# Attention with a decaying causal mask inside a one-core layer: wider transposed scores, wider products with V, a mask at the diagonal tiles alone

## The reference, cut to what matters

```python
Q, K, V = ...                                  # 2 x 16 heads, each 512 x 16
S = jnp.einsum('hid,hjd->hij', K, Q) * SCALE   # row i by K, column j by Q
delta = idx[:, None] - idx[None, :]
decay = jnp.where(delta < 0, 0.0, -delta.astype(jnp.float32) ** ALPHA)   # ALPHA = 1
S = jnp.where(delta < 0, -jnp.inf, S) + decay
C = jax.nn.softmax(S, axis=-1)
attn = jnp.einsum('hij,hjd->hid', C, V)
```

## Time and profile before

| | us |
|---|---|
| median of 3 runs | 376.57 (376.19 to 376.78) |
| span of the profiled execution | 374.3 |
| PE, DVE, ACT, POOL busy | 261.6, 257.6, 167.8, 142.4 |

### The profile page before, as it was taken

The page is one execution under the profiler, slowest core; times in us unless marked ns, Lnnn a source line. Parts: engine busy times, 40 slices in busy tenths (PEclk is TensorE's granted clock), DMA queues, the critical chain, the costliest instruction groups (busy, mean ns, idle before and its releaser), DMA issues.

```text
span 374.3 us, 7052 instructions
## 1 busy us (share of the span) xinstructions
PE 261.6 (70%) x2080; PEld 200.1 (53%) x2080; DVE 257.6 (69%) x833; ACT 167.8 (45%) x412; POOL 142.4 (38%) x212
## 2 busy tenths in 40 slices
PE   1715652999993179769999999998619429999900
PEld 0504541998982058515445455466418319898800
DVE  5798463587874787797788888446676406787726
ACT  2850352455554126325666776767142105565400
POOL 6390684177875004372000000000007733877730
PEclk9975887699998559955999999999956859999965
DMA  5999593544530704853333221000002232545227
GB/s 158 389 227 188 165 331 116 183 151 139 159 109 3 223 1 121 250 157 103 87 87 87 73 60 43 1 2 2 1 2 77 104 116 87 164 132 166 82 91 246
DMA packets 33931, 45.66 MB, mean 122 GB/s; under 512 B 5869, under 2 KB 27475, under 8 KB 33896
## 3 DMA queue, kind: packets, MB, share of 16 engines
q1 hardware_dynamic: 29304, 36.25, 34.6%
q0 software_dynamic: 4592, 8.98, 7.0%
HBM read 28.06 MB, written 20.61 MB: 130 GB/s over the span
## 4 chain that ended last, share of the span: by engine, by line
PE 34%; DMA 19%; POOL 15%; DVE 13%; issue 10%; SPq 5%; ACT 4%; POOLq 0%; DVEq 0%; ACTq 0%
PE bank L295 15%; POOL slots_x L512 8%; DMA slots_x<-zeros 7%; POOL results L526 5%; PE bank L922 5%; DMA xb<-slots_x 5%; PE bank L880 4%; DVE bank L1275 3%; DMA yg<-results 2%; DMA stk_q<-parts_d 2%; PE bank L831 2%; PE bank L901 2%; SPq L414 2%; DVE res L1197 1%; PE bank L740 1%
## 5 line engine op out<-in xcount | busy, mean ns | idle before, releaser
L526 POOL DMA_INDIRECT results<-ysb,yi x62 | 61.0, 984 | 31.3 <-DVE ysb L1178 17.1
L1275 DVE CUSTOM_DVE_ANT_0 bank<-bank,dec 128x512 f32<-128x512 f32 (+3 forms) x128 | 60.6, 510 | 14.6 <-PE bank L880 13.6
L512 POOL DMA_INDIRECT slots_x<-xn,slot x32 | 31.8, 993 | 33.6 <-DVE slot L1118 12.9
L586 ACT ACTIVATE sg<-bank 128x128 f32<-128x128 f32 x78 | 21.6, 277 | 51.3 <-PE bank L295 51.3
L880 PE MATMUL bank<-stk_q,stk_k 96*128 96x512 bf16 (+3 forms) x128 | 39.3, 340 | 6.8 <-DVE mmax L1275 4.8
L1166 DVE TENSOR_TENSOR xT_l<-bank,xT_h 128x256 fp32r<-128x256 f32 x62 | 26.4, 425 | 24.0 <-ACT xT_h L625 23.9
L295 PE MATMUL bank<-wh,xT_h 128*128 x124 | 41.8, 337 | 0.8 <-DVE xT_l L1166 0.8
L625 ACT ACTIVATE xT_h<-bank 128x256 fp32r<-128x256 f32 x62 | 23.8, 384 | 38.8 <-PE bank L831 37.9
L831 PE MATMUL bank<-ident,xb 128*128 128x128 f32 x124 | 25.8, 293 | 20.4 <-DMA xb<-slots_x 19.8
L712 ACT ACTIVATE ct<-bank,dec 128x512 f32<-128x512 f32 x64 | 34.8, 581 | 7.7 <-PE bank L901 7.5
L504 POOL COPY xn<-to_row 128x4 int32<-128x4 int32 x8 | 2.3, 289 | 93.7 <-DVE xn L1059 93.7
(11 more groups left out here) (173 smaller groups left out, 729.9 us busy)
## 6 DMA issues: line engine op xcount, KB each, us to landing
xb<-slots_x SPq DMA_DIRECT2D x62, 128.5 KB
w_raw<-in_experts SPq DMA_DIRECT2D x17, 384.0 KB, 6.4
yg<-results SPq DMA_DIRECT2D x16, 256.0 KB, 4.5
slots_x<-zeros SPq DMA_DIRECT2D x1, 3983.5 KB, 27.6
parts_d<-part SPq DMA_DIRECT2D x6, 384.0 KB, 2.8
stk_k<-parts_d SPq DMA_DIRECT2D x8, 192.0 KB, 3.4
stk_q<-parts_d SPq DMA_DIRECT2D x8, 192.0 KB, 3.5
res<-in_x SPq DMA_DIRECT2D x4, 256.0 KB, 3.7
```

What stands on the lines that cost most here:

```text
L512: pool.indirect_dma_start(slots_x, where, xn[:, t, :], None)\
L526: pool.indirect_dma_start(results, where, ysb[c % RING][:], None, bounds_check=4 * N - 1, oob_is_err=False).then_inc(s_ys[c % RING], 16)
L1275: dve.tensor_tensor_reduce(s_i, s_i, dec[:, SEQ - w:SEQ], 1.0, NEG, ALU.add, ALU.max, mmax[g % 2][:, n % G * QT + i:n % G * QT + i + 1])\
```

## The change

The decay comes from six rows in place of three, chosen so that they hold for every pair of tiles: three with the place in a tile and the tile number of i, three with those of j. So a transposed tile row can be one matmul that starts at its own diagonal tile: 512, 384, 256 and 128 columns. Entries above the diagonal are hidden by a second matmul that adds `hide` (0 or -3e38) to the diagonal tiles alone. The steps of a head are now tile row 0 (bank 2); rows 3 and 1 (bank 3); row 2 (bank 4). The columns that the array takes for a head are the same: 512 + 512 + 512 + 256 = 1792 before, and (512 + 128) + (128 + 384 + 256) + (256 + 128) = 1792 now, in 7 matmuls in place of 8. The banks' sizes and the three exponentials stay; none has a bias from memory now.

`ct` now holds a tile row's diagonal tile and what is behind it side by side, so a product with V is one matmul for each tile row and head: 4 pieces of 512, 384, 256 and 128 columns, in place of 7, at three places of the loop in place of six. The columns are the same: 1280 for each head.

The rows are built at the start in two small tiles, by four instructions on POOL (`place_k`, `place_q`) and four DMAs that write into them and wait for POOL (`s_place`); `hide` takes two more instructions on POOL. Of ACT's three copies at the end of the first shared expert two are left. The stack is 104 rows high (`STD`) in place of 101, and `decay_rows` writes 6 and 8 rows in place of 3 and 5.

```diff
-    STD = STM + 3
+    STD = STM + 6
...
+        t_tiles = [(0,), (3, 1), (2,)]
+        ct_at = {0: 0, 3: 512, 1: 640, 2: 1024}
...
-            at = SEQ + 1
-            sp.dma_start(masks_s[:, 0:P], masks[:, at:at + P]).then_inc(s_msk, 16)
-            sp.dma_start(masks_s[0:3, P:P + SEQ], masks[0:3, at + P:at + P + SEQ]).then_inc(s_msk, 16)
-            sp.dma_start(masks_s[32:37, P:P + SEQ], masks[3:8, at + P:at + P + SEQ]).then_inc(s_msk, 16)
+            at = SEQ + 1 + P
+            sp.wait_ge(s_place, 2)
+            for to in (place_k[0:3, :], place_q[5:8, :]):
+                sp.dma_start(to[0:2, :], masks[0:2, at:at + SEQ]).then_inc(s_msk, 16)
+                sp.dma_start(to[2:3, :], masks[6:7, at:at + SEQ]).then_inc(s_msk, 16)
...
+            link(pool.memset(place_k[:], -1.0))
+            link(pool.memset(place_q[:], 1.0))
+            pool.affine_select(out=place_k[:], in_=place_k[:], compare_op=ALU.not_equal, fill=-1.0 * P, base=-5,
+                               pattern=[[0, SEQ]], channel_multiplier=1).then_inc(s_place, 1)
+            pool.affine_select(out=place_q[:], in_=place_q[:], compare_op=ALU.not_equal, fill=1.0 * P, base=-4,
+                               pattern=[[0, SEQ]], channel_multiplier=1).then_inc(s_place, 1)
...
+            link(pool.memset(hide[:], 0.0))
+            pool.affine_select(out=hide[:], in_=hide[:], compare_op=ALU.is_ge, fill=NEG, base=0,
+                               pattern=[[1, P]], channel_multiplier=-1).then_inc(s_hide, 1)
...
-                    act.activation(ct[n % 6][:, a:b], bank[2 + i][:, 0:b - a], ACT.Exp, bias=dec_b if i else 0.0)\
-                        .then_inc(s_exp, 1)
+                    act.activation(ct[n % 6][:, a:b], bank[2 + i][:, 0:b - a], ACT.Exp).then_inc(s_exp, 1)
...
-                if i == 0:
-                    pe.matmul(bank[2][:], ident_b[:], dec_d[:, None, :].to_broadcast([P, QT, P]), start=True,
-                              stop=False, skip_group_check=True)
-                    for j in range(QT):
-                        tile = slice(j * P, (j + 1) * P)
-                        mm = pe.matmul(bank[2][:, tile], q[0:STM, u, tile], k[0:STM, u, tile], start=False,
-                                       stop=True, skip_group_check=True)
-                else:
...
+                at, to, tiles = 0, bank[2 + i], t_tiles[i]
+                for j in tiles:
+                    pe.matmul(to[:, at:at + SEQ - j * P], q[:, u, j * P:(j + 1) * P], k[:, u, j * P:SEQ],
+                              start=at == 0, stop=False, skip_group_check=True)
+                    at += SEQ - j * P
+                n_d = len(tiles)
+                pe.matmul(to[:, 0:n_d * P], ident_b[:], hide[:, None, :].to_broadcast([P, n_d, P]), start=False,
+                          stop=True, skip_group_check=True).then_inc(s_st, 1)
...
-            v_steps = {(0, 1): ((0, False),), (0, 2): ((0, True),), (0, 3): ((1, False),),
-                       (1, 0): ((1, True),), (1, 1): ((2, False), (2, True)), (1, 2): ((3, False),)}
+            v_steps = {(0, 1): (0,), (0, 3): (1,), (1, 1): (2, 3)}
```

More of the change, by code:

```diff
@@ L92, in macaron_kernel @@
         eps = sb("eps", [P, 1])
[L93 to L97, removed]
+        dec = sb("dec", [P, SEQ])
+        hide = sb("hide", [P, P], BF16)
+        rows_k = sb("rows_k", [6, SEQ], BF16)
+        rows_q = sb("rows_q", [8, SEQ], BF16)
         qkb = sb("qkb", [P, 2, KT])
@@ L133, in macaron_kernel @@
         r0 = ExitStack()
-        masks_s = sb("masks_s", [P, P + SEQ], F32, r0)
+        place_k = sb("place_k", [6, SEQ], F32, r0)
+        place_q = sb("place_q", [8, SEQ], F32, r0)
         r0.close()
@@ L244, in macaron_kernel @@
         s_msk = sem("s_msk")
+        s_place = sem("s_place")
+        s_hide = sem("s_hide")
         s_dcy = sem("s_dcy")
@@ L376, in blocks @@
                         sp.dma_start(wa_raw[j][:], w).then_inc(s_was[j], 16)
-                    sp.dma_start(dec[:], masks[:, 0:at]).then_inc(s_dcy, 16)
+                    sp.dma_start(dec[:], masks[:, 0:SEQ]).then_inc(s_dcy, 16)
                 with sp.Fori(0, NB // RING - 1) as n:
@@ L432, in attention @@
                 load_stacks(1)
-                sp.wait_ge(s_row, 3)
+                sp.wait_ge(s_row, 2)
                 for i in range(3):
@@ L613, in ffn @@
                 if f == 0:
[L614 to L617, removed]
+                    act.wait_ge(s_msk, 64)
+                    act.activation(rows_k[:], place_k[:], ACT.Copy).then_inc(s_row, 1)
+                    act.activation(rows_q[:], place_q[:], ACT.Copy).then_inc(s_row, 1)
                 def step(b, live):
@@ L910, in maxima_turn, with times_v @@
                              ident_b[:]).then_inc(s_mt, 1)
[L912 removed]
+            def times_v(g, j):
                 c, hg = g // 4, g % 4
[L915 removed]
+                if j == 0:
                     pe.wait_ge(s_exp, 3 * G * (g + 1))
@@ L918, in times_v @@
                         pe.wait_ge(s_ot, g)
-                lo, hi, at = ((j + 1) * P, SEQ, off[j]) if behind_it else (j * P, (j + 1) * P, j * P)
+                lo, at = j * P, ct_at[j]
                 for u in range(G):
                     n, h = G * g + u, G * hg + u
-                    mm = pe.matmul(bank[6][32 * u:32 * u + 32, lo:hi], V[:, c * QT + j, h * VW:h * VW + 32],
-                                   ct[n % 6][:, at:at + hi - lo], start=j == 0, stop=not behind_it,
+                    mm = pe.matmul(bank[6][32 * u:32 * u + 32, lo:SEQ], V[:, c * QT + j, h * VW:h * VW + 32],
+                                   ct[n % 6][:, at:at + SEQ - lo], start=j == 0, stop=j == QT - 1,
                                    skip_group_check=True)
@@ L964, in _ @@
             pe.wait_ge(s_pr, 8)
-            pe.wait_ge(s_row, 1)
+            pe.wait_ge(s_hide, 1)
             def project(t):
@@ L986, in _ @@
                     if n >= G:
-                        for j, behind_it in v_steps.get((n % G, i), ()):
-                            times_v(n // G - 1, j, behind_it)
+                        for j in v_steps.get((n % G, i), ()):
+                            times_v(n // G - 1, j)
                 if n == NH + 3:
```

3 lines of the change are left out of this document (removed).

## The result

| | us |
|---|---|
| changed kernel, 20 runs | 372.62 (369.18 to 376.81) |
| kernel before, 20 runs beside them | 376.96 (374.66 to 380.05) |
| ratio | 0.9884, 95% interval 0.9858 to 0.9910 |
| span of the profiled execution | 370.9, 3.4 less |
| PE, DVE, ACT, POOL busy | 259.8, 255.5, 160.5, 145.7 |

The kernel is faster, and the median is 0.2 us from the forecast of 372.4. Medians and ranges here are of all runs, while a ratio and its interval leave out runs over 1.5% above the fastest of their kernel, so a ratio need not be the quotient of two medians.

The account below looks back on a forecast made before the run. PE and DVE together bound a group of four heads, next the stack load; -2.25 (five loop marks) - 2.0 (loop's end) + 0.1 (start) = -4.1 us, from 376.57 to 372.4; own range 371.6 to 373.4.

Parts of the forecast that it names:

- The price of a run: Each unbroken run of products with V costs PE 0.25 us beside its columns; three fewer save 0.75 us a group.
- Rival 4: The 0.25 us comes again within wider matmuls, so only the exponentials gain, -0.4: 376.2 us, no change; chance 0.06.
- The engines' floor: In the head loop, PE and DVE would allow a group of 10.49 - 0.75 = 9.74 us.
- Load + 3.6: A loop group can't be shorter than its stack load plus 3.6 us: 9.8 for a load of 6.2.
- Rival 1: All stack loads in the loop take 7.4 us: 373.9 us, or 374.6 with the first mark late too; chance 0.12.
- rival 2: No stack load in the loop is late, because they come down to 6.0 us: -5.6, 370.9 us; chance 0.10.
- The end of the loop: Where no stack is loaded: 1.45 us less from products of two groups and 0.53 from exponentials, 2.0 us in all.
- the 0.70 for the stretch from 243: At the loop's end, the second group's products, with the output projection between two pieces, were counted as 0.70 us less.
- The start: Before the fill, four DMA issues in place of three and SP's wait for POOL: +0.1 us, ends -0.1 and +1.4.
- The decay rows: SP's six DMAs of them from 157.97 cost 0 more with more rows; upper end 4.0 us more.
- Rival 3: The issues of the decay rows' DMAs grow with their rows, -4.1 + 4.0: 376.5 us, no change; chance 0.05.
- rival 5: TensorE's clock falls to 1.2 GHz in stack waits, some 9 us more a group: 381 us, slower; chance 0.06.

Follow-up runs that it names:

- ACT's version: The changed kernel with the three DMAs for stk_q of groups 3 to 7 issued by ACT beside SP's three: 377.33 us, ratio 0.9934.
- the kernel with POOL's queue: The changed kernel with the three DMAs for stk_q of groups 3 to 7 issued by POOL beside SP's three: 381.3 us, ratio 1.0073.

## Why the prediction was right, point by point

**The price of a run.** 0.25 us from rows where four matmuls stood beside eight; 0.247 measured from the loop's pace, 10.44 against 9.70. That it belongs to the run, not to the matmul, was argued from one x16 row and is now shown by the old kernel with three runs, whose 28 narrow matmuls take as long as the 16 wide ones. Rival 4 (the price comes again within wider matmuls) is out: the 512-column piece took 0.99, which the line had given.

**The engines' floor.** 9.74 forecast, 9.70 measured without loads and with four stacks, and for the longer first group 10.0 and 9.94. Of the 0.80 less, 0.74 are the runs; 0.06 (10.50 to 10.44) are the new form of the transposed scores and the exponentials, for which the forecast had 0 with bounds of 0.05.

**Load + 3.6.** Right to 0.1 us in all groups of the changed kernel, and in ACT's version. What was wrong is the length of the loads. The step counted with each group's own load from the trace of before, 7.45 for stack 4 and 6.2 to 6.6 for others, as if a slow load belonged to its place. It doesn't: the loads are 7.2, 6.3, 6.8, 6.9, 6.3 now. So the marks came out otherwise than forecast, one by one: +0.08 where 0.75 less stood (stack 3's last DMA took 4.1 us to land, 3.3 before), 1.16 less where nothing stood, 0.10 less for 0.3, 0.01 less for 0.6, 0.57 less for 0.6. The sum is off by less, since the draws offset each other: 1.76 less in place of 2.25. That the sum came this near is partly luck. PE's waits were 0.4 to 1.2 us where 0.3 to 0.6 was said, from the same step. One load for all groups gives the measured pace, 5 x (6.7 + 3.6) = 51.5, but 6.7 is the mean of the changed kernel's own loads; the five in the trace of before have 6.6, which makes 51.1, hardly nearer than the forecast's 51.0. Rival 1 (7.4 for all) and rival 2 (6.0, none late) lie outside what appeared, 6.3 to 7.2.

**The end of the loop.** 2.0 forecast, 1.56 measured. The exponentials' part was 0.53, and everything that isn't a run came to 0.48. The runs' part was 1.45 and came to 1.08. The term that was too large is the 0.70 for the stretch from 243. With the turning of the maxima as the dividing point, the first group's runs came to 0.74 (0.75 forecast) and this stretch's to 0.34. There the output projection and ACT's exponentials stand between the pieces; what took the other half is not shown.

**The start.** +0.1 forecast. The first stack load of the loop came 0.07 earlier, which says little, since executions differ there by up to 6 us (177.0 to 183.2); what is read is the queue. SP comes to the first of the four DMAs at the old time, doesn't wait, and the fill is issued at 10.86 as before:

```profile
5.25 0.33 SPq L348 DMA_DIRECT2D place_k<-in_masks  x1
...
10.86 0.70 SPq L353 DMA_DIRECT2D slots_x<-zeros  x1
```

**The decay rows.** No cost, as forecast; the first issue takes 0.92 where it took 0.90, and the other five 0.70 to 0.76 with 6 and 8 rows, where they took 0.76 to 0.81 with 3 and 5. Rival 3 is out.

**The clock, rival 5.** Not in this kernel: the granted clock stayed 1.00 through its stack waits. (The first group's window has 0.95, but from the stretch ahead of its wait: 0.60 from 178 to 180, and 1.00 from there on.) A fall does happen, though, and showed in the kernel with POOL's queue, behind waits of 1.76 and 1.99. There it cost 1.1 to 1.3 us of PE in a group, not the 9 that I had put on it. The waits' length alone doesn't decide: 2.19 us with ACT's queue, and 1.76 in the old kernel with three runs, left the clock where it was. What does is open.

**Sum.** The span fell by 3.4 (forecast 4.1), the median by 4.3 in the runs of the result and by 2.7 in the later ones. That the median came within 0.2 us of the forecast is partly luck: the parts add up to 0.7 less. The forecast also said that a measurement can tell 0.2%, from three runs within 0.6 us; the twenty lie within 5.4 us, and the interval of their ratio is 0.5% wide.

## What to carry to other kernels

Where narrow matmuls in another tiling stand between wide ones, count the unbroken runs, not the matmuls: put them together as long as the engine that eats the wide ones' output has enough in its banks to go on, and no further. When the engines of a loop get faster, its floor becomes release-to-use of the buffers, mark to mark; ask for one more buffer before asking for another queue. A time that hangs on a DMA's landing is a draw from a spread: forecast with the mean of all its rows, not with the row at that place, and take the range from their spread.

## What the runs showed of the hardware

- A run of products with V, whose output is 32 partitions high, cost 0.247 us beside its columns at a granted clock of 1.00 (groups of 10.44 us with six runs, 9.70 with three). It took the same time with 4 matmuls of 512 columns as with 8 narrower ones, 1.06 and 1.07 us.
- Two queues that load the same stack at once: SP's landings went from 3.1 to 3.5 us to 5.4 to 6.4 with POOL beside it, for the same stack, and to 5.3 to 6.6 with ACT, in the loads issued from 188 and from 198. Fewer issues ahead of them bought nothing.
- PE's granted clock was 0.86 and 0.89 over two groups with one wait of 1.76 and 1.99 us in each, and 1.00 over two others with waits of 1.76 and 2.19.
- When no stack is late the loop repeats to 0.01 us: 9.70 four times in a row, with loads into four stacks and with none.
